# Multi-head attention over 16 batches: the steps of all batches as one stream

## The reference, cut to what matters

```python
x = ft.reshape(B, N, C)                         # 16 batches, 1024 tokens, 512 channels, float32
qkv = (x @ w_qkv + b_qkv).reshape(B, N, 8, 192)
q, k, v = jnp.split(qkv, 3, axis=-1)            # 8 heads of 64
attn = softmax(einsum('bxhd,byhd->bxyh', q, k) * 64 ** -0.5, axis=2)
res = einsum('bxyh,byhd->bxhd', attn, v).reshape(B, N, 512)
out = res @ w_out + b_out + x
```

## Time and profile before

| | us |
|---|---|
| median of 3 runs | 4104.45 (4103.89 to 4105.86) |
| profiled execution, time | 4103.61 |
| profiled execution, span | 4101.8 |
| busy in the span: PE, DVE, ACT, POOL | 3915.1, 2721.0, 2707.0, 1769.3 |
| TensorE clock granted | 1.00 of full speed |

### The profile page before, as it was taken

One profiled execution on the slowest core, in us unless ns is written; L12 is line 12 of the kernel. 1 busy time (PEld: TensorE's weight loads), 2 busy tenths in 40 slices (PEclk: granted clock), 3 DMA queues, 4 the chain that ended last, 5 costly groups with the idle time before them and its releaser, 6 DMA issues.

```text
span 4101.8 us, 105442 instructions
## 1 busy us (share of the span) xinstructions
PE 3915.1 (95%) x38156; PEld 3113.8 (76%) x38156; DVE 2721.0 (66%) x4395; ACT 2707.0 (66%) x2965; POOL 1769.3 (43%) x888
## 2 busy tenths in 40 slices
PE   6999999999999999999999999999999999999999
PEld 5777777777777777777777777777777777777777
DVE  5757757577575775757667576675766757667576
ACT  4756847568475774757757477574775747657476
POOL 1534525345253552535525255352553525435254
PEclk9999999999999999999999999999999999999999
DMA  3011021110202102020021211202011121110201
GB/s 98 22 54 42 20 76 25 57 39 17 79 22 70 26 20 76 22 74 22 25 71 24 71 24 28 68 22 73 22 37 58 25 71 25 38 58 22 63 22 43
DMA packets 100845, 179.85 MB, mean 44 GB/s; under 512 B 16192, under 2 KB 16192, under 8 KB 100288
## 3 DMA queue, kind: packets, MB, share of 16 engines
q1 hardware_dynamic: 100288, 172.29, 14.9%
HBM read 71.57 MB, written 33.55 MB: 26 GB/s over the span
## 4 chain that ended last, share of the span: by engine, by line
PE 68%; DVE 17%; issue 11%; ACT 1%; DVEq 1%; POOL 1%; DMA 0%; SPq 0%; ACTq 0%; POOLq 0%
PE psum L472 31%; PE psum L503 9%; PE psum L532 6%; PE psum L534 6%; DVE max_parts L749 6%; PE psum L556 4%; PE psum L560 4%; PE psum L558 4%; DVE q_shift L728 3%; DVE k_lo_hi L726 3%; DVE p_lo L771 2%; PE psum L486 2%; DVE q_shift L762 2%; ACT p_hi L655 1%; POOL p_lo L380 1%
## 5 line engine op out<-in xcount | busy, mean ns | idle before, releaser
L380 POOL TENSOR_TENSOR p_lo<-p_full,p_hi 128x1024 f16<-128x1024 f32 x752 | 1607.3, 2143 | 2069.7 <-ACT p_hi L655 2069.7
L749 DVE TENSOR_REDUCE max_parts<-psum 128x1 f32<-128x512 f32 x2048 | 1341.3, 686 | 516.7 <-PE psum L503 507.8
L654 ACT ACTIVATE p_full<-psum,prob_bias 128x1024 f32<-128x1024 f32 x1024 | 1144.1, 1117 | 384.8 <-PE psum L534 371.1
L655 ACT ACTIVATE p_hi<-psum,prob_bias 128x1024 f16<-128x1024 f32 x1024 | 1137.2, 1111 | 0.0
L556 PEld LDWEIGHTS psum<-v_parts,p_hi 128*128 128x128 f16 x8192 | 743.8, 98 | 263.2 <-issue 161.8
L556 PE MATMUL psum<-v_parts,p_hi 128*128 128x65 f16 x8192 | 857.2, 193 | 35.5 <-DVE o_heads L781 19.9
L558 PE MATMUL psum<-v_parts,p_hi 128*128 128x64 f16 x8192 | 850.7, 192 | 0.0
L560 PE MATMUL psum<-v_parts,p_lo 128*128 128x65 f16 x8192 | 848.0, 194 | 0.0
L532 PE MATMUL psum<-q_hi_hi,k_lo_hi 128*128 128x512 f32 x2048 | 818.7, 400 | 1.9
L503 PE MATMUL psum<-k_lo_hi,q_hi_hi 128*128 128x512 f32 x2048 | 769.3, 429 | 51.7 <-DVE q_shift L728 21.5
L534 PE MATMUL psum<-q_shift,k_shift 128*128 128x512 f32 x2048 | 802.3, 392 | 0.0
(11 more groups left out here) (61 smaller groups left out, 4269.8 us busy)
## 6 DMA issues: line engine op xcount, KB each, us to landing
x_in<-in_x SPq DMA_DIRECT2D x128, 256.0 KB, 3.9
k_shift<-k_lo_hi SPq DMA_DIRECT2D x256, 128.0 KB, 2.2
q_hi_hi<-q_hi_hi SPq DMA_DIRECT2D x256, 128.0 KB, 2.3
y_tile<-in_x SPq DMA_DIRECT2D x128, 256.0 KB, 2.8
result<-y_tile SPq DMA_DIRECT2D x128, 256.0 KB, 2.8
o_heads<-in_L_conv_w_qkv SPq DMA_DIRECT2D x12, 256.0 KB, 4.1
o_heads<-in_L_conv_w_out SPq DMA_DIRECT2D x4, 256.0 KB, 4.1
out_bias<-in_L_conv_b_out SPq DMA_DIRECT2D x1, 256.0 KB, 5.8
```

Of the source, the lines that this page charges most:

```text
L380: nc.gpsimd.tensor_tensor(p_lo[:, s % P_SLOTS, :, :], p_full[:, s % 2, :, :], p_hi[:, s % P_SLOTS, :, :], ALU.subtract).then_inc(p_lo_read ...
L654: nc.scalar.activation(p_full[:, s % 2, :, :], score_banks(s), ACT.Exp, scale=SCALE, bias=prob_bias[:, :])
L655: nc.scalar.activation(p_hi[:, s % P_SLOTS, :, :], score_banks(s), ACT.Exp, scale=SCALE, bias=prob_bias[:, :]).then_inc(exp_done, 1)
L749: nc.vector.reduce_max(max_parts[:, u % 2, q_tile, k_half:k_half + 1], max_bank(w), AX.X).then_inc(max_tile_done, 1)
```

## The change

The steps of all 16 batches are one stream of slots (16 x 64), the fills of a batch being given slots relative to its own first step: x transposes in -17 to -10, v in two groups of four heads (256 columns) in -14 to -1 and 11 to 31, q/k of head h from 8h-11, output transposes in 62 to 72, projections in 66 to 103. So a slot of the loop body holds fills of two batches (`rels`), and the code is three runs: the start of the first batch, the loop, the end of the last. Fills use banks 3 and 7, assigned by a table at build time; scores use banks 0 to 2, one tile each, and a score tile waits for the exp of the tile three earlier. ACT does exp one tile (512 columns) at a time, with transposes' and q/k's high parts between the two tiles of a step. Every kind of work has semaphores of its own. x has two buffers, y three, p_hi four, p_lo two; the output transposes have three buffers of their own. POOL takes steps 0, 1, 2, 4, 5, 6 of 8 (before 0, 2, 3, 4, 6, 7). On SP the copy of q goes ahead of that of k, and y_load(t+3) follows y_store(t).

Sizes, slots and banks:

```diff
-X_SLOTS, Y_SLOTS, P_SLOTS = 4, 4, 3
-SCORE_BANKS = (0, 1, 2, 3)
-FILL_BANK_STEADY = 7
-PV_BANK = 6
...
+UNIT = 4
+STEPS = UNITS * UNIT
+KEYS_PER_STEP = 2
+X_SLOTS, Y_SLOTS, O_SLOTS, HI_SLOTS, LO_SLOTS = 2, 3, 3, 4, 2
+V_GROUP = HEADS // 2
...
+SCORE_BANKS, PV_BANK, RING_BANKS, FILL_BANKS = (0, 1, 2), 6, (4, 5), (3, 7)
...
+X_TRANSPOSE_SLOT = (-17, -16, -15, -13, -12, -12, -11, -10)
+O_TRANSPOSE_SLOT = (62, 64, 65, 67, 68, 69, 70, 72)
+PROJECT_PARTS = (((66, 0, TERMS),), ((67, 0, TERMS),), ((68, 0, TERMS),), ((69, 0, TERMS),), ((71, 0, TERMS),),
+                 ((74, 0, 6), (76, 6, TERMS)), ((99, 0, 6), (100, 6, TERMS)), ((103, 0, TERMS),))
+V_SLOT = ((-14, -13, -9, -6, -5, -4, -3, -1), (11, 15, 18, 20, 23, 26, 28, 31))
+Y_BIAS_SLOT = (54, 56, 58, 67, 69, 71, 73, 76)
...
+def qk_parts(h, half):
+    begin = 8 * (h - 1)
+    if half == 1:
+        return [(begin, 0, 6), (begin + 1, 6, TERMS)]
+    if h == 2:
+        return [(begin - 2, 0, TERMS)]
+    return [(begin - 3, 0, 4), (begin - 2, 4, TERMS)]
...
+MAX_TILES = (((0,), (1,)), ((2,), (3,)), ((4, 5), (6,)), ((7,), ()))
...
+EMPTIED_AFTER = {"qk": 1.7, "v": 1.0, "project": 1.1, "x_transpose": 0.8, "o_transpose": 0.8}
...
+        if first == 0:
+            of[b, w] = FILL_BANKS[0] if w == ("project", 6) else min(FILL_BANKS, key=lambda k: free[k])
+        free[of[b, w]] = STEPS * b + c + (EMPTIED_AFTER[w[0]] if last == TERMS else STEPS)
...
+POOL_STEPS = (0, 1, 2, 4, 5, 6)
...
+def slots(batches):
+    return {"first": [(c, (0,)) for c in range(FIRST_SLOT, LOOP_SLOT)],
+            "loop": [(c, (0, 1)) for c in range(LOOP_SLOT, LOOP_SLOT + STEPS)],
+            "last": [(c, (0,)) for c in range(LOOP_SLOT, LAST_SLOT + 3)]}[batches]
```

The load of y on SP, and what a score tile waits for on PE:

```diff
+            def y_load(b, t):
+                if t >= Y_SLOTS:
+                    wait_for(sp, y_stored[t - Y_SLOTS], b, 16, 16)
+                else:
+                    last = max(u for u in range(TOKEN_TILES) if u % Y_SLOTS == t)
+                    wait_for(sp, y_stored[last], b, 16, 0)
+                sp.dma_start(y_tile[:, t % Y_SLOTS, :], x_tok[b, t * P:(t + 1) * P, :]).then_inc(y_loaded[t], 16)
...
+                for n in range(KEYS_PER_STEP):
+                    tile = KEYS_PER_STEP * s + n
+                    wait_for(pe, exp_done, i, SCORE_TILES, SCORE_TILES * r + tile + 1 - tiles_since(tile))
```

The order of a slot on PE:

```diff
+            def run(i, part):
+                for g, rels in slots(part):
+                    for r in rels:
+                        for w in ring_early(g - STEPS * r):
+                            ring(i, r, w)
+                    for r in rels:
+                        for w in transposes_of_slot(g - STEPS * r):
+                            transpose(i, r, w)
+                    for r in rels:
+                        for piece in fills_of_slot(g - STEPS * r):
+                            fill(i, r, *piece)
+                    if step_of(g + 1, rels) is not None:
+                        step_scores(i, g + 1)
+                    for r in rels:
+                        for w in ring_late(g - STEPS * r):
+                            ring(i, r, w)
+                    if step_of(g - 1, rels) is not None:
+                        step_pv(i, g - 1)
```

ACT:

```diff
+            def exp_tile(i, g, n):
+                s = g % STEPS
+                if n == 0:
+                    if g >= 2 or not isinstance(i, int):
+                        wait_low(act, i, g - 2)
+                    wait_for(act, pv_done, i, STEPS, g + 1 - HI_SLOTS)
+                wait_for(act, scores_ready, i, SCORE_TILES, KEYS_PER_STEP * g + n + 1)
+                nc.scalar.activation(p_full[:, s % 2, n, :], scores(s, n), ACT.Exp, scale=SCALE, bias=prob_bias[:, :])
+                nc.scalar.activation(p_hi[:, s % HI_SLOTS, n, :], scores(s, n), ACT.Exp,
+                                     scale=SCALE, bias=prob_bias[:, :]).then_inc(exp_done, 1)
...
+            def run(i, part):
+                for g, rels in slots(part):
+                    if step_of(g, rels) is not None:
+                        exp_tile(i, g, 0)
+                    for r in rels:
+                        for w in transposes_of_slot(g - STEPS * r):
+                            transposed_hi(i, r, w)
+                    for r in rels:
+                        for w in completed_in_slot(g - 1 - STEPS * r):
+                            if w[0] == "qk":
+                                qk_hi(i, r, w)
+                    if step_of(g, rels) is not None:
+                        exp_tile(i, g, 1)
+                    for r in rels:
+                        for w in completed_in_slot(g - STEPS * r):
+                            if w[0] == "v":
+                                v_hi(i, r, w)
```

DVE:

```diff
+            def run(i, part):
+                for g, rels in slots(part):
+                    for r in rels:
+                        for w in ring_early(g - STEPS * r):
+                            row_max_part(i, r, w)
+                    if step_of(g - 2, rels) is not None and (g - 2) % UNIT == UNIT - 1:
+                        unit_output(i, g - 2)
+                    for r in rels:
+                        for w in transposes_of_slot(g - STEPS * r):
+                            transposed_lo(i, r, w)
+                    for r in rels:
+                        for w in completed_in_slot(g - 1 - STEPS * r):
+                            if w[0] == "qk":
+                                qk_lo(i, r, w)
+                    if step_of(g, rels) is not None and not on_pool(g):
+                        step_lo(i, g)
+                    for r in rels:
+                        for w in ring_late(g - STEPS * r):
+                            if w[0] == "row_max":
+                                row_max_part(i, r, w)
+                            else:
+                                shift_rows(i, r, w)
+                    for r in rels:
+                        for w in completed_in_slot(g - STEPS * r):
+                            if w[0] == "v":
+                                v_lo(i, r, w)
+                            elif w[0] == "project":
+                                project_add(i, r, w)
```

## The result

The changed kernel takes 4078.2 us (median of 4 runs, 4074.8 to 4081.5), the kernel before 4105.0 in 4 runs beside it (4103.9 to 4105.9). The ratio is 0.9935, 95% interval 0.9918 to 0.9952: 27 us faster, where 109 were forecast. The profiled execution took 4080.7 with a span of 4078.8.

The account below looks back on a forecast made before the run. PE was taken as the bound: 239.1 us of stream plus 6.0 of waits make 245.1 a batch; 16 batches, adjusted for uncovered ends and start, give a span of 3992 and a time of 3995 us, range 3900 to 4115.

Parts of the forecast that it names:

- Waits that stay: PE's remaining waits, added slot by slot through each queue: 6.0 us a batch, giving 245.1 a batch, 8.9 less than before.
- v at 256 columns: v matmuls on PE, 192 of 256 columns instead of 96 of 512: 0.125 us each, 24.0 instead of 21.9 a batch.
- rival 3: v matmuls of 256 columns bound by their weight load, 0.19 to 0.228 us each: 4195 to 4312 us; chance 0.05.
- Exp of 512 columns: ACT's exp by single banks, four instructions a step for two: 0.58 us each, a step 2.32 instead of 2.00, covered by PE.
- rival 2: ACT becomes the bound: short exp costs 0.70 us, a step 2.80, 8.5 more a batch, 4131 us; chance 0.12.
- slot 48: x transpose 1 on PE waits for the bank of q/k (7, 0), which ACT reaches behind x transpose 0: 1.5 us.
- slot 43: The next unit's first row maximum waits 0.7 us for DVE's q/k low part; with shift and rest 1.6.
- slot 34: A slot like slots 42 to 44, where PE waits behind ACT and DVE work: 0.9 us a batch.
- Rival 1: Fewer waits: the list's four waits mostly hidden, 240.1 us a batch instead of 245.1, 3915 us in all; chance 0.17.
- The wait for an x load: In slot 53, x transpose 6 waits for a load issued 3.4 us before: 0 to 1.3 us, taken as 0.5.
- The ends: Uncovered work at the stream's start and end, seventeen slots of the first batch and the last batch's projections: about 38 us each.
- Rival 4: The waits only move: DVE's order within a slot holds PE, 11 to 17.4 us a batch, 4075 to 4177 us; chance 0.11.

## Why the prediction was right or wrong

**The step that failed** is "Waits that stay", and its sum, "6.0 of waits: 245.1 a batch". The list went slot by slot through the queues as if slot followed slot without a seam. But the end of PE's loop body came to lie in the middle of the stream, behind a PV step of 0.73 us, and its branch and the half clock behind it were given no cost. They cost 5.2 us a batch, 71 us in all by the version with PE written out; the edges of ACT, DVE and POOL, left out of the sum too, are 7.5 more. Of the 83 us between forecast and measurement that leaves 5. The row was there to be read: the branch of 4.8 us stands in the trace of before under its line. There it looked free since the batch's last wide matmuls covered 3.6 us of it and DVE's own edge lay beside the rest; the kernel before without PE's loop, being no faster, agrees with that. The change left it 0.4 us of short matmuls as cover, and DVE's edge, still beside it, is over first (1233.3 against 1234.2). For the work of ACT, DVE, POOL and SP the prediction names what covers it; it does not mention a branch of any engine. The prediction's own sign for being wrong, PE waiting over 10 us a batch, came true: 250.8 - 239.1 = 11.7.

**What was right.** Without PE's loop the period is 245.6, forecast 245.1, and the time 4007.3, forecast 3995. Of the 12 between, 7.5 go with the edges of the other three engines (3999.8 without them), and some 3 us of the rest lie at the ends (below).

*v at 256 columns*, forecast 0.125: the changed kernel's twelve take 1.44 from first to next, 0.12 each. The bounds of 0.114 to 0.228 were right, and the half-price one was near:

```profile
1109.23 0.28 PE L479 MATMUL psum<-wqkv_hi,xT_hi 128*128 128x256 f32 x1
...
1110.67 0.40 PE L536 MATMUL psum<-q_hi_hi,k_lo_hi 128*128 128x512 f32 x1
```

So rival 3 falls. *Exp of 512 columns*, forecast 0.58: 0.57 from start to start, where half of the 1.00 of the earlier trace rows would be 0.50; ACT's timeline of the changed kernel:

```profile
1101.07 0.68 ACT L642 ACTIVATE p_hi<-psum,prob_bias 128x512 f16<-128x512 f32 x1
1101.64 0.69 ACT L641 ACTIVATE p_full<-psum,prob_bias 128x512 f32<-128x512 f32 x1
```

ACT is busy for 189.6 us a batch against a forecast 184, and rival 2 falls. So a step pays 4 x 0.57 - 2 x 1.00 = 0.28 for two instructions more, 0.14 each. The Trainium skill (Perfetto Trace Analysis, Optimizing Scalar/DVE Operations), which the prediction weighed, is right that smaller operations cost more; its 51 ns is under the 0.14 seen here. PE covers it.

*The waits of the list*: slot 48 has 1.28 by the row (forecast 1.5), and the loopless version without it is 17 us faster, 1.1 for each of 15. The row maximum in slot 43 waits 0.6 a batch for the low part of q (forecast 0.7) and the one in slot 35 another 0.7 (forecast 0.9, as slot 34). Rival 1 falls with that: they were not hidden. PE's waits in the one batch from 1011.0, without the issue, sum to about 3.8 by the view of waits, and 6.0 was the forecast; waits under 0.17, by which a record overlaps the next, don't show there, and the others are short by as much. The wait for an x load was put at 0.5 a batch, for x transpose 6 in slot 53; the changed kernel shows

```profile
PE psum L494 <- DMA x_in<-in_x: 9.9, 14, 2.4
```

Of the 9.9, 4.0 are two waits before the first scores; the other twelve come to 0.4 a batch. They stand one slot earlier than forecast, in slot 52 at x transpose 5, whose load is issued behind transpose 3.

*The ends*, forecast 38 each: 40.2 from the first transpose to the first score, 38.6 from the last PV to the end.

**Rival 4** contains the measured time (4075 to 4177), but not for its reason: it said that DVE's order within a slot holds PE, and with DVE's order untouched and PE's loop gone the time is 4007.

One reading of the trace of before was off, without bearing on the sum: the wait of 1.43 us at 1099.89, taken as one of those in every head, comes once a batch (20.4 us in 16 times on DVE's row maximum, by the view of waits), so what makes up the 1.3 us of a head was not shown.

## What to carry to other kernels

Cost the loop's own branch like any other instruction, on every engine, and look at what is queued ahead of it on its engine: a branch that is hidden by the seam of a batch shows up when the seam is filled. Put the edge where many long instructions stand ahead of it and no wait stands between them and the branch, or write the engine that bounds the kernel out without a loop: 71 us were won so in the changed kernel, and 10 lost in the kernel before, where DVE's edge stood beside PE's. A wait seen in one batch is not a wait in every batch: take its count from the view of waits before multiplying.

## What the runs showed of the hardware that was not expected

A taken branch on PE's sequencer took 3.3 to 5.0 us (medians 3.5 in the changed kernel, 4.8 before) and 0.08 when not taken. PE ran on under it for as long as matmuls were queued: 16 wide ones started after the branch had begun in the kernel before (1045.7 to 1049.2), 11 with the edge behind projection 1, and 14 short ones, worth 0.4 us, in the changed kernel. The other engines' branches have short records, but on ACT and DVE the loop body's first instruction comes late as well. The edges of both in the changed kernel, beside the one of PE shown above:

```profile
L665 ACTq COMPARE_BRANCH  x1: 45/45/45, 1226.9 to 1226.9; - x1
L665 ACTq FUSED_REGOPS  x1: 50/50/50, 1229.6 to 1229.6; - x1
...
L812 DVEq COMPARE_BRANCH  x1: 62/62/62, 1230.5 to 1230.5; - x1
L812 DVEq FUSED_REGOPS  x1: 63/63/63, 1233.3 to 1233.3; - x1
```

That is 2.7 us on ACT and 2.8 on DVE; over the 14 edges 2.4 to 2.8 and 2.8 to 3.2, and on POOL 0.3.

Idle PE did not always bring the clock down. At twelve of the changed kernel's 14 edges, 7 to 13 matmuls behind the gap start some 0.43 apart, at half clock; at two, with gaps of 3.26 and 3.27 us between those of the others (3.10 to 3.73), the full clock stays. One of the two, by PE's timeline and by windows (columns as above; the window shown at 1231.00 has 0.81):

```profile
1479.91 0.39 PE L536 MATMUL psum<-q_hi_hi,k_lo_hi 128*128 128x512 f32 x1
...
1485.22 0.49 PE L504 MATMUL psum<-k_lo_hi,q_hi_hi 128*128 128x512 f32 x1 [3.26 <-issue]
...
1487.39 0.39 PE L536 MATMUL psum<-q_hi_hi,k_lo_hi 128*128 128x512 f32 x1
```

```profile
1482.00:1491.00 9.00, 5.78 (x48) 4.70 (x48) 2.53 (x5) 4.03 (x7) 2.68 (x2) 1.00 0.03 6
```

This tells idle and half clock apart at the same gap. The step with the edge lasts 7.48 and 7.51 at the two, 8.66 to 9.80 at the twelve, and 4.03 without an edge: at the two the gap costs its length and 0.2, 3.5 us; at the twelve the half clock costs 1.3 to 1.8 on top of that. After gaps of 1.43 to 1.74 us (the edge behind projection 1) the clock stayed full at all 13 edges, and in the kernel before with PE written out it fell at three of 15 seams, after waits of 1.85 to 1.93, and not after one of 1.87. So the length of the gap alone does not say whether the clock falls; what does was not tested.
